# Post-layernorm attention and gated FFN on one core: q and k projected three batches ahead, own tiles for v's input

## The reference

```python
def _layernorm(x, axis=-1, eps=1e-05): ...            # mean and variance over the last axis
# x: (32, 256, 128); 16 heads of 8 features
q, k, v = (split_heads(x @ w.T) for w in (wq, wk, wv))
attn = einsum('bhqd,bhkd->bhqk', q, k) / sqrt(8)
attn = attn + slopes[None, :, None, None] * -abs(pos_k - pos_q)      # ALiBi
attn = softmax(attn, axis=-1)
out = merge_heads(einsum('bhqk,bhkd->bhqd', attn, v)) @ wo.T + bo
x = _layernorm(x + out)
# ternary weights with a scale per output, 128 -> 512 -> 512 -> 512 -> 128
h = silu(tlin(x, w1)) * tlin(x, w2)
h = gelu(tlin(h, h1))
h = gelu(tlin(h, h2))
x = _layernorm(x + tlin(h, w3))
```

## Time and profile before

| | us |
|---|---|
| median of 3 runs | 1440.05 (1439.1 to 1441.06) |
| profiled execution | 1441.41 |
| its span | 1439.3 |
| PE busy | 887.5 (62%) |
| DVE busy | 685.0 (48%) |
| ACT busy | 617.3 (43%) |
| POOL busy | 239.7 (17%) |

### The profile page before, as it was taken

One profiled execution on the slowest core, in us unless ns is written; L12 is line 12 of the kernel. 1 busy time (PEld: TensorE's weight loads), 2 busy tenths in 40 slices (PEclk: granted clock), 3 DMA queues, 4 the chain that ended last, 5 costly groups with the idle time before them and its releaser, 6 DMA issues. The chain is left out here.

```text
span 1439.3 us, 26150 instructions
## 1 busy us (share of the span) xinstructions
PE 887.5 (62%) x8322; PEld 610.2 (42%) x8322; DVE 685.0 (48%) x1405; ACT 617.3 (43%) x1102; POOL 239.7 (17%) x405
## 2 busy tenths in 40 slices
PE   2544445555544445555544445555569999999996
PEld 1322223333322223333322223333336888888885
DVE  3444334444443334444443334444436776776775
ACT  2233223333332223333332223333346777777774
POOL 1111111222121111121221111121220000000001
PEclk9987777787877777787877777787779999999999
DMA  3222222121112222121212222122210111111101
GB/s 111 56 61 77 71 58 73 56 59 55 55 55 77 66 56 73 56 59 55 55 55 74 69 56 73 56 59 63 62 45 26 37 34 33 44 36 29 44 23 37
DMA packets 111619, 80.66 MB, mean 56 GB/s; under 512 B 15392, under 2 KB 98464, under 8 KB 111584
## 3 DMA queue, kind: packets, MB, share of 16 engines
q1 hardware_dynamic: 110704, 77.32, 18.8%
q0 software_dynamic: 880, 2.88, 0.7%
HBM read 45.82 MB, written 33.55 MB: 55 GB/s over the span
## 5 line engine op out<-in xcount | busy, mean ns | idle before, releaser
L624 DVE TENSOR_REDUCE negmax<-ps_a 128x2 f32<-128x512 f32 x512 | 334.1, 685 | 576.8 <-PE ps_a L400 576.0
L546 ACT ACTIVATE probs<-ps_b 128x512 f32<-128x512 f32 x512 | 284.3, 597 | 673.9 <-PE ps_b L400 671.4
L385 PE MATMUL ps_a<-qk_stack 52*128 52x256 bf16 x1024 | 215.1, 302 | 519.1 <-DMA qk_stack<-mrow 445.8
L385 PEld LDWEIGHTS ps_a<-qk_stack 52*128 52x128 bf16 x1024 | 70.6, 100 | 618.7 <-issue 371.9
L393 PE MATMUL ps_b<-qk_stack 55*128 55x256 bf16 x1024 | 213.8, 300 | 4.8 <-ACT probs L546 3.1
L441 PE MATMUL ps_o<-probs,v_aug 128*32 128x256 f32 x2048 | 163.7, 446 | 0.0
L400 PE MATMUL ps_a<-corner_sb,eye_sb 64*128 64x128 bf16 x1024 | 153.6, 236 | 0.0
L400 PE MATMUL ps_b<-corner_sb,eye_sb 64*128 64x128 bf16 x1024 | 152.5, 234 | 0.0
L876 ACT ACTIVATE gelu_f<-ps_r,sc 128x512 f32<-128x512 f32 x128 | 88.3, 690 | 79.7 <-PE ps_r L817 72.2
L689 POOL CAST mrow<-mrest 16x128 bf16<-16x128 f32 x64 | 17.9, 280 | 603.9 <-DVE mrest L598 603.9
L400 PEld LDWEIGHTS ps_a<-corner_sb,eye_sb 64*128 64x128 bf16 x1024 | 107.1, 106 | 11.7
(11 more groups left out here) (101 smaller groups left out, 1449.0 us busy)
## 6 DMA issues: line engine op xcount, KB each, us to landing
qk_stack<-qk_scratch SPq DMA_DIRECT2D x128, 192.0 KB, 3.4
qk_scratch<-qk_sb SPq DMA_DIRECT2D x64, 192.0 KB, 2.2
qk_scratch<-qk_sb SPq DMA_DIRECT2D x64, 128.0 KB, 2.1
qk_stack<-mrow SPq DMA_DIRECT2D x384, 2.0 KB
xT_sb<-in_xT SPq DMA_DIRECT2D x32, 128.0 KB, 2.1
x_sb<-in_x SPq DMA_DIRECT2D x32, 128.0 KB, 2.1
qk_scratch<-qk_sb SPq DMA_DIRECT2D x64, 64.0 KB, 1.8
x_scratch<-x_sb SPq DMA_DIRECT2D x32, 128.0 KB, 1.7
```

The source lines that it names most:

```text
L385: pe.matmul(ps_a[A_BANK[h]][:, qb * SEQ:(qb + 1) * SEQ], q_stack[par][rows_of, j, qb * P:(qb + 1) * P], k_stack[par][rows_of, j, :], start ...
L546: nc.scalar.activation(probs[:, h % HALF, :], ps_b[k % 2][:], ACT.Exp, scale=slope[h]).then_inc(exp_done, 1)
L624: nc.vector.tensor_reduce(negmax[:, k // HALF, k % GROUPS, k % HALF // GROUPS, :], ps_a[A_BANK[k]][:].rearrange("p (b k) -> p b k", b=BLK) ...
```

## The change

The steps begin at -3 instead of -2, and the loop covers steps 3 to 26. In step t batch t+3 is projected, from xT_sb[1-s]; the counts of qk_done, qk_first, qk_left, qk_split and spilled on PE, ACT, DVE and POOL move by one. SP's spill and stack in step t are still those of batch t+2. v is projected from tiles of its own, xv_sb, with a semaphore xv_landed; xT_sb is loaded four batches ahead, as soon as qk_done allows it. In SP's queue the stack of half 1 stands ahead of the loads, the store of x1 behind the spill, and in the steps before 0 both halves are stacked at once.

```diff
@@ -216,6 +216,7 @@
         probs = sb("probs", [P, HALF, BLK * SEQ])
         v_aug = [sb(f"v_aug{i}", [P, BLK, HEADS, VCOLS]) for i in range(2)]
         xT_sb = [sb(f"xT_sb{i}", [P, SEQ]) for i in range(2)]
+        xv_sb = [sb(f"xv_sb{i}", [P, SEQ]) for i in range(2)]
         x_sb = [sb(f"x_sb{i}", [P, BLK, D]) for i in range(2)]
         xb_sb = [sb(f"xb_sb{i}", [P, BLK, D]) for i in range(2)]
         negmax = sb("negmax", [P, 2, GROUPS, HH, BLK])
@@ -242,7 +243,7 @@
         rows_landed = sem("rows_landed")
         rows_laid = [sem(f"rows_laid{i}") for i in range(2)]
         v_laid = sem("v_laid")
-        xT_landed, x_landed = sem("xT_landed"), sem("x_landed")
+        xT_landed, xv_landed, x_landed = sem("xT_landed"), sem("xv_landed"), sem("x_landed")
         qk_done, qk_first, qk_left = sem("qk_done"), sem("qk_first"), sem("qk_left")
         qk_second, qk_split = sem("qk_second"), sem("qk_split")
         spilled = sem("spilled")
@@ -263,12 +264,15 @@
         raw_hi, lo_seen = sem("raw_hi"), sem("lo_seen")
 
 
+        STEPS = dict(first=-3, loop_from=3, loop_to=BATCH - 5, last=BATCH + 1, unroll=2)
+        FIRST = STEPS["first"]
+
         pieces = []
         for (hi, lo), src in zip(wts, raw_w):
             kt, n = src.shape[1:]
             for a in range(0, kt, HID // n):
                 pieces.append(tuple(w[:, a:a + HID // n, :] for w in (hi, lo, src)))
-        piece_at = [(-2, 8)] * RAW_BUFS + [(0, 11), (1, 11), (2, 11), (BATCH - 3, 11), (BATCH - 2, 11),
+        piece_at = [(FIRST, 8)] * RAW_BUFS + [(0, 11), (1, 11), (2, 11), (BATCH - 3, 11), (BATCH - 2, 11),
                                            (BATCH - 1, 4), (BATCH - 1, 10)]
         assert len(pieces) == N_PIECES == len(piece_at)
 
@@ -281,9 +285,6 @@
             return raw[:, n % RAW_BUFS, :].rearrange("p (k n) -> p k n", n=width)
         N_CONST, N_QK_CONST = 6, 3
 
-
-        STEPS = dict(first=-2, loop_from=3, loop_to=BATCH - 3, last=BATCH + 1, unroll=2)
-        FIRST = STEPS["first"]
 
         block = ctx.enter_context(nc.Block())
 
@@ -296,8 +297,12 @@
             sp.dma_start(rows_sb, rows).then_inc(rows_landed, DMA)
             for dst, src in ((eye_f, eye), (corner_f, corner), (id_sb, ident), (wv_sb, wvT), (wo_sb, woT), (bo_sb, bo)):
                 sp.dma_start(dst[:], src).then_inc(const_landed, DMA)
-            sp.wait_ge(xT_landed, DMA)
-            sp.dma_start(xT_sb[1][:], xT[1]).then_inc(xT_landed, DMA)
+            for i in range(2):
+                if i:
+                    sp.wait_ge(xT_landed, DMA)
+                    sp.dma_start(xT_sb[i][:], xT[i]).then_inc(xT_landed, DMA)
+                    sp.wait_ge(xv_landed, DMA)
+                sp.dma_start(xv_sb[i][:], xT[i]).then_inc(xv_landed, DMA)
             sp.dma_start(x_sb[0][:], x[0].rearrange("(a p) d -> p a d", p=P)).then_inc(x_landed, DMA)
 
             def stack(b, par, hf):
@@ -330,32 +335,39 @@
                                      mrow[hf][r][g * HH * BLK:(g + 1) * HH * BLK, :]).then_inc(m_landed[hf], DMA)
 
             def step(t, s):
-                if live(t, BATCH) and live(t + 2, BATCH):
-                    wait_apart(sp, v_done, t + 1, passed["sp"])
-                    wait_apart(sp, xT_landed, (t + 2) * DMA, passed["sp"])
-                    sp.dma_start(xT_sb[s][:], xT[t + 2]).then_inc(xT_landed, DMA)
-                if live(t + 1, BATCH):
+                if live(t + 1, BATCH) and live(t - 1, BATCH):
                     wait_apart(sp, spilled, (t + 2) * len(SPILLS) * DMA, passed["sp"])
                     wait_apart(sp, scores_b, t * HEADS, passed["sp"])
                     stack(t + 1, 1 - s, 1)
+                if live(t, BATCH) and live(t + 2, BATCH):
+                    wait_apart(sp, v_done, t + 1, passed["sp"])
+                    wait_apart(sp, xv_landed, (t + 2) * DMA, passed["sp"])
+                    sp.dma_start(xv_sb[s][:], xT[t + 2]).then_inc(xv_landed, DMA)
+                if live(t + 2, BATCH) and live(t + 4, BATCH):
+                    wait_apart(sp, qk_done, t + 3, passed["sp"])
+                    wait_apart(sp, xT_landed, (t + 4) * DMA, passed["sp"])
+                    sp.dma_start(xT_sb[s][:], xT[t + 4]).then_inc(xT_landed, DMA)
                 if live(t, BATCH):
                     max_rows(t, s, 1)
-                if live(t - 3, BATCH):
-                    wait_apart(sp, x1_done, t - 2, passed["sp"])
-                    wait_apart(sp, x1_stored, (t - 3) * DMA, passed["sp"])
-                    sp.dma_start(x1_dram[t - 3], x1_sb[1 - s][:]).then_inc(x1_stored, DMA)
                 if live(t + 2, BATCH):
                     wait_apart(sp, qk_split, t + 3, passed["sp"])
                     if live(t, BATCH):
                         wait_apart(sp, stacked[0], (t + 1) * GROUPS * DMA, passed["sp"])
                         wait_apart(sp, stacked[1], (t + 1) * GROUPS * DMA, passed["sp"])
                     spill(s)
+                if live(t - 3, BATCH):
+                    wait_apart(sp, x1_done, t - 2, passed["sp"])
+                    wait_apart(sp, x1_stored, (t - 3) * DMA, passed["sp"])
+                    sp.dma_start(x1_dram[t - 3], x1_sb[1 - s][:]).then_inc(x1_stored, DMA)
+                if live(t + 2, BATCH):
                     wait_apart(sp, spilled, (t + 3) * len(SPILLS) * DMA, passed["sp"])
                     if live(t, BATCH):
                         wait_apart(sp, scores_b, t * HEADS + HALF, passed["sp"])
                     if isinstance(t, int) and t < 0:
                         sp.wait_ge(rows_laid[s], 2)
                     stack(t + 2, s, 0)
+                    if isinstance(t, int) and t < 0:
+                        stack(t + 2, s, 1)
                 if live(t + 1, BATCH):
                     max_rows(t + 1, 1 - s, 0)
                 if live(t + 1, BATCH) and live(t, BATCH):
@@ -449,8 +461,8 @@
                 pe.transpose(ps[0:BLK * HALF, 0:P], negmax[:, hf, :, :, :].rearrange("p g h a -> p (g h a)"),
                              id_sb[:]).then_inc(mT_done, 1)
 
-            def project(t, s, n, w):
-                return pe.matmul(ps_m[0][:, n * SEQ:(n + 1) * SEQ], w[:], xT_sb[s][:], start=True, stop=True,
+            def project(par, n, w):
+                return pe.matmul(ps_m[0][:, n * SEQ:(n + 1) * SEQ], w[:], xT_sb[par][:], start=True, stop=True,
                                  skip_group_check=True)
 
             def step(t, s):
@@ -466,7 +478,7 @@
                 for k in range(HEADS):
                     scores(t, s, k)
                     if k == 1 and live(t, BATCH):
-                        wait(pe, qk_left, min(t + 2, BATCH) if isinstance(t, int) else t + 2)
+                        wait(pe, qk_left, min(t + 3, BATCH) if isinstance(t, int) else t + 3)
                         turn_max(ps_m[0], t, 1)
                     if k == 1 and live(t - 2, BATCH):
                         wait(pe, oT_copied, t - 1)
@@ -482,20 +494,20 @@
                                 mm = pe.transpose(ps_m[1][:, (qb * 2 + j) * P:(qb * 2 + j + 1) * P],
                                                   o_sb[:, j, qb * P:(qb + 1) * P], id_sb[:])
                         mm.then_inc(o_turned, 1)
-                    if k == 5 and live(t + 2, BATCH):
-                        wait(pe, xT_landed, (t + 3) * DMA)
+                    if k == 5 and live(t + 3, BATCH):
+                        wait(pe, xT_landed, (t + 4) * DMA)
                         if live(t, BATCH):
                             wait(pe, m_left, t * 2 + 2)
                         else:
-                            wait(pe, qk_left, t + 2)
+                            wait(pe, qk_left, t + 3)
                         if isinstance(t, int) and t == FIRST:
                             pe.wait_ge(wq_scaled, 1)
-                        project(t, s, 0, wqs_sb)
+                        project(1 - s, 0, wqs_sb)
                     if k == 9 and live(t + 1, BATCH):
                         wait(pe, normed, t)
-                        wait(pe, xT_landed, (t + 2) * DMA)
+                        wait(pe, xv_landed, (t + 2) * DMA)
                         for tb in range(BLK):
-                            mm = pe.matmul(ps_m[1][:, SEQ + tb * D:SEQ + (tb + 1) * D], xT_sb[1 - s][:, tb * P:(tb + 1) * P],
+                            mm = pe.matmul(ps_m[1][:, SEQ + tb * D:SEQ + (tb + 1) * D], xv_sb[1 - s][:, tb * P:(tb + 1) * P],
                                            wv_sb[:], start=True, stop=True, skip_group_check=True)
                         mm.then_inc(v_done, 1)
                         turn_max(ps_m[1], t + 1, 0)
@@ -507,8 +519,8 @@
                         for qb in range(BLK):
                             mm = pe.transpose(ps_m[1][:, qb * P:(qb + 1) * P], o_norm[:, qb, :], id_sb[:])
                         mm.then_inc(oT_done, 1)
-                    if k == 13 and live(t + 2, BATCH):
-                        project(t, s, 1, wk_sb).then_inc(qk_done, 1)
```

(22 more changed lines are left out.)

## The result

| | us |
|---|---|
| median before, in the comparison | 1439.94 (4 runs) |
| median with the change | 1025.12 (4 runs, 1020.23 to 1027.35) |
| ratio | 0.7114 (95% interval 0.7085 to 0.7143) |
| profiled execution | 1020.23, its span 1018.4 |

The account below looks back on a forecast made before the run. Bound: PE idling 14.4 us a batch behind SP's spill, which waits for POOL's split. Start 44.7 + 31 x 19.0 = 633.7, plus tail 392.8, gave span 1026.5 and, adjusted for profiling, 1027 us; range 995 to 1062.

Parts of the forecast that it names:

- The wait before the spill: In SP's queue, a wait of 12.8 us for POOL's split of q and k; claimed to go, with PE's 14.4.
- Two paths meet at the rows of half 0: Before each batch's row transfers, compute and SP's queue both finish; low clock: rows landed at T + 19.7 and T + 19.1.
- Batches of both kinds: PE's clock at batch starts: some low (19.7 us a batch), some high (18.4); 19.0 us taken.
- a clock that stays up in every batch: Rival, PE's clock: short waits leave it high, batches of 18.4 us, 1009 us in all; chance 0.22.
- The start: Before batch 0: its rows no longer follow a spill, so PE starts it at 44.7 us, 12 us earlier.
- The tail: From batch 31's start to the end of the span: the same work as before, 392.8 us.
- xv's load hidden: SP's added load per batch, 0.38 us and a 0.2 gap, is covered by SP's wait for the maxima.
- x1's store free: SP's store of x1, 0.38 us, falls inside the spill's 1.56 us landing and costs nothing.
- Head 8: Half 1's rows land at T + 9.0, PE reaches head 8 at T + 10.4: no wait, barely.
- Late landings: Rival, spill and stack loads: transfers land later, at worst 20.4 us a batch, up to 1071 us; chance 0.18.
- Slower: Rival, SP's wait for the spill's landing: 14.3 us more a batch would give 1474 us; chance 0.02.
- the chain unbroken: Rival: another wait still ties the spill to its own step's projection, time stays near 1440 us; chance 0.03.

## Why the prediction held, point by point

- **The wait before the spill goes, and the 14.4 us with it.** Right. The run with all but the projection has the time of before, so nothing else took it away.
- **Two paths meet at the rows of half 0.** Right, and both are seen: in the batch from 328.18 SP starts them 0.10 us behind POOL's split (T + 13.44), in the one from 346.81 it starts 0.18 behind its own stack loads (T + 13.29). I had 13.1 for SP's path at the full clock, and a batch of 18.4; the batch from 346.81 took 18.58. The difference is at the beginning of that path. SP's rows of half 1 wait for POOL's split of them, which I let come 0.7 us earlier at the full clock (T + 2.9); they started at T + 3.26, 0.4 earlier than before the change. From there to the rows of half 0 it took 10.03 us, where I had 10.2.
- **Batches of both kinds, 19.0 us.** The mean is 18.80. The clock was full behind some waits and low behind others, as taken. But I had priced two kinds, 18.4 and 19.7, and the second as if the clock were low from T on. It fell only after T, so the slower batches took 18.60 to 19.48, and the split of half 0's rows came at T + 13.3 to 14.0 instead of T + 14.37. The rival of a clock that stays up in every batch (1009 us) fell, and with it what follows here from the rule that the clock falls only once the engine has sat idle for a whole stretch (the Trainium skill, TensorE: Matmul & The Clock Gate, Part 1): behind waits of the same 1.75 us it was 0.67 at 178.20 and 1.00 at 309.63. The term that was off most is this mixture: 31 x 0.2 = 6 us.
- **The start.** 44.7 us forecast, 44.70 measured. **The tail** after batch 31's start: 392.8 forecast, 390.9 measured. **Around the span:** 2.1 and 1.8.
- **The 2 us are in part luck.** For the profiled execution the sum said 1028.6, and it took 1020.23: 8.4 us less, 6.2 of it from the batches, 1.9 from the tail and 0.3 around the span. The sum also took the profiled execution to be 1.4 us above the median; it was 4.9 below it, and that gives back 6.3.
- **xv's load hidden, x1's store free.** Right: one more load changes nothing. The store is free only where it was put; ahead of the spill it costs 18 us.
- **Head 8: no wait, barely.** Wrong by a little: in about every third batch PE waits there for the rows of half 1, mostly 0.48 or 0.76 us. About as much was waited there for ACT in any case, so it counts for little.
- **Late landings.** They didn't come where something waits. The Trainium skill's 2 us for an access to HBM at high load (DMA: Bandwidth & Descriptors, Latency and other measured facts) had given, as an estimate, 1.8 us more per landing. With the mean traffic up from 56 to 83 GB/s the spills landed as before, and the stack loads had the same median, 3.4 us. Whether 83 GB/s is a high load in the Trainium skill's sense, no run shows. The loads of xT did land later, in the median 2.7 us after their issue instead of 2.1, and nobody was waiting for them. That is the order, not the traffic: behind the stack loads, but at the pace of before (the run with all but the projection), it was 2.9, and ahead of them at the new pace (the old order in the queue) 2.2. The spills:

```profile
DMA to landing us min/median/max: 1.8/2.1/3.4
```

- **Slower, or the chain unbroken.** Neither.

## What to carry to other kernels

The transfer that a trace names at a wait is only the last link: walk the issuing queue backwards until something in it waits for an engine, and ask whether that work could have been done a round earlier. When such a wait goes, the queue's own walk is next, so price every issue and gap in it (a row transfer of 2 KB held SP's queue for 0.64 us, a load of 128 KB for 0.4) and put what nobody waits for inside a landing that must be waited for anyway. Then look for a second queue: three of six small transfers moved to another engine's queue gave 5% on top.

## What I had not expected of the hardware

- Behind waits of 1.75 to 2.52 us the granted clock fell in some batches and not in others at the same length, and often only about 1 us after PE had begun again (numbers above); no run here shows what decides it. In the run with two more transfers, behind waits of 3.2 to 3.3 us, it fell in all batches of the loop but one. Without waits at the rows PEclk reads 9 in the first 24 slices, up to the last batch.
- A row transfer held POOL's queue for 0.524 us in the median and SP's for 0.635, and the two queues issued side by side: three rows took 2.03 to 2.05 us on SP and 1.56 to 1.67 on POOL, there 0.59 behind the split, where six on SP took 4.09. On ACT three of them took 1.96 us, and the exponential behind them waited, although at the other half of the same batch two ACT instructions (342.24 and 342.71) overlapped the issues from 342.08 on.
- With transfers on POOL's queue the first matmul of the FFN comes later: PE's gap ahead of it was 6.39 us with the change, 9.32 with rows on POOL and 6.64 with rows on ACT. It is 3 of the 14.5 us by which the version with q and k two ahead and rows on POOL gained less than forecast (there the gap was 9.12 us, and 6.18 before). The trace shows the place: POOL begins the last layernorm of the attention later, held by its own queue, with the change and with rows on POOL:

```profile
651.20 0.23 POOL L167 TENSOR_SCALAR vareps<-meanvar 128x2 f32<-128x2 f32 x1 [1.69 <-POOLq L191]
```

```profile
602.63 0.23 POOL L167 TENSOR_SCALAR vareps<-meanvar 128x2 f32<-128x2 f32 x1 [4.87 <-POOLq L191]
```

That idle time of POOL is 4.87 us in all three versions with rows on POOL's queue, and 1.69 before, with the change and with rows on ACT. What the queue does in it, no run shows.
